# Expert blocks of three and of four token tiles in a routed feed-forward layer

## The chip, the core and the metric

The kernel runs on one core of a Trainium2 chip, as one program. Its time is the device time in microseconds from start to end, and lower is better. The core has five engines with a queue of instructions each: TensorE (PE, with its weight loads shown apart as PEld), VectorE (DVE), ScalarE (ACT), GpSimd (POOL) and SyncE (SP). They wait for one another by semaphores. PSUM, where TensorE writes, has eight banks of 512 fp32 columns.

## The reference

A graph layer is followed by a feed-forward layer with eight experts, of which each token takes one. The change touches the second alone:

```python
T = 20000 tokens, D = 256, F = 1024, E = 8
C = ceil(1.25 * T / E)                                # 3125 places of an expert
logits = layernorm(x) @ gate_w + gate_b
idx = argmax(softmax(logits));  prb = its probability
pos = (cumsum(one_hot) * one_hot).sum(-1) - 1         # rank of a token in its expert
kept = pos < C
buf[idx, pos] = layernorm(x) where kept
hmid = relu(einsum('ecd,edf->ecf', buf, w1) + b1)
ybuf = einsum('ecf,efd->ecd', hmid, w2) + b2
out = x + nan_to_num(ybuf[idx, pos] * (prb * kept))
```

How many tokens an expert gets depends on the data. A token tile is 128 tokens, so an expert has at most 25 of them.

## The kernel before

The program has three stages: edges and nodes (to about 380 us), routing (to about 550 us) and the experts.

**Routing** works over 160 node tiles. VectorE counts how many tokens each expert got, turns this into a number of tiles per expert, and that into a number of blocks. With `BT = 3`, an expert with `t` tiles gets `t // 3 + 1` blocks (`tiles_43`, `tiles_third`: times 43, shifted right by 7), the first `3 * blocks - t` of which are narrow and hold two tiles, the others wide with three. An expert is raised to `LEAST_TILES = 8` tiles, and 9 become 10. `first_block` holds where each expert begins, `first_wide` where its wide blocks begin. A slot table has `NST` slots, `BT` for each of the `NB` blocks that there can be at most, 64 x 3 = 192. It is built in ten steps (`in_row`, `in_tile`, `in_code` on VectorE, then 16 matmuls into `ps_code` on TensorE) and becomes `idx_row` (which rows each slot gathers) and `put_row` (which rows it is added to). Slots without a token read a spare row and are added to spare rows.

**The experts** (`expert_block`) run one loop over narrow blocks and one over wide ones for each expert, with bounds that are read from the two tables. Each matrix is held as a sum of a high and a low part, so a product takes three matmuls. In a block `b`:

- GpSimd (one loop over all blocks) gathers block `b + 2`: for each of `BT` tiles an indirect DMA for the rows (`xg`) and one for their statistics and probability (`sg`). It starts when ScalarE has taken the last ones. Then it adds block `b - 1` to the output, `BT` indirect DMAs (`add_rows`). It does this for all `BT` tiles, in narrow blocks too.
- TensorE does the up projection `up`, for each of 8 slices `f` six matmuls over all the block's columns into one of four `ps_h` banks (`SLOTS = 4`), then the down projection `down` in four steps `j`, for each tile six matmuls of 256 columns into `ps_y`. After the first step it transposes the next block (`turn`, `2 * BT` transposes).
- ScalarE empties each `ps_h` bank twice (`h_hi` and `h_all`, with relu and bias). Between the slices it scales the previous block's rows (`scale_rows`, after `f = 1`) and normalises the next block (`normalise`, after `f = 3`), and at the end takes `x_hi`, the high part of the transposed rows.
- VectorE makes `h_lo` from `h_all - h_hi` for each pair of slices, `x_lo`, and replaces infinities and NaNs of the block before (`find_infinite`, `add_infinities`, `keep_finite`); `add_infinities` waits until the earlier `add_rows` has landed. Last it adds `ps_y` and the bias into `y_sum`.

In each expert's first wide block ScalarE and VectorE also split the next expert's weights in high and low parts (`split_high`, `split_own`, `split_low`).

A narrow block leaves out the third tile in `up`, `down`, the relus, `h_lo` and `y_sum` alone.

## Time and profile before

| | us |
|---|---|
| median of 3 runs | 1450.41 |
| lowest and highest | 1445.53, 1452.19 |
| profiled execution | 1453.49 |
| its span (first to last instruction) | 1451.7 |
| TensorE busy in it | 1221.9 (84%) |
| GpSimd busy | 1016.1 (70%) |
| VectorE busy | 1004.8 (69%) |
| ScalarE busy | 957.3 (66%) |

### The profile page before, as it was taken

The page shows a single profiled execution, that of the slowest core. Times are in us where ns is not written, and L with a number is a line of the kernel's source. Part 1 is how long each engine was busy: PE and PEld are TensorE (multiplying, and loading weights), DVE is VectorE, ACT ScalarE, POOL GpSimd, SP SyncE. Part 2 cuts the span into 40 slices and gives each one's busy share as a digit, 9 for nine tenths or more (in the row PEclk, how much of TensorE's full clock was granted, in tenths as well). Part 3 has the DMA queues.
Part 4 walks back from the last instruction along what each step waited for, and adds up shares of the span by engine and source line. Part 5 has one row for each costly group of instructions (what it writes and reads, how often), then busy time and mean ns, then how long its engine had stood idle before and what let it go on. Part 6 is the DMA issues. An engine that isn't in the chain of part 4 may idle for free.

```text
span 1451.7 us, 26791 instructions
## 1 busy us (share of the span) xinstructions
PE 1221.9 (84%) x7872; PEld 1070.8 (74%) x7872; DVE 1004.8 (69%) x2147; ACT 957.3 (66%) x2128; POOL 1016.1 (70%) x920
## 2 busy tenths in 40 slices
PE   2477678887499343999999999999999999999993
PEld 0244335555366143999999999999999999999993
DVE  7999997986499893755757655755755575556653
ACT  4788896885266363766767666766666776667662
POOL 7788688766477304777777766777776777778785
PEclk9977767999799676999999999999999999999997
DMA  9889976444666202423433422433422342233333
GB/s 331 236 266 284 287 203 145 72 70 49 163 218 216 93 10 84 106 47 48 103 48 55 105 44 47 104 52 49 107 47 44 48 109 48 47 45 55 51 55 41
DMA packets 131884, 153.54 MB, mean 106 GB/s; under 512 B 17164, under 2 KB 118604, under 8 KB 131680
## 3 DMA queue, kind: packets, MB, share of 16 engines
q0 software_dynamic: 51648, 64.60, 27.2%
q1 hardware_dynamic: 58512, 66.59, 14.2%
q10 hardware_dynamic: 21648, 21.49, 4.3%
q8 instruction: 29, 0.48, 0.1%
q14 instruction: 47, 0.39, 0.1%
HBM read 98.82 MB, written 53.81 MB: 105 GB/s over the span
## 4 chain that ended last, share of the span: by engine, by line
PE 52%; issue 4%; POOL 3%; ACT 2%; DMA 1%; DVE 0%; ACTq 0%; POOLq 0%; DVEq 0%
PE f_ps_y L1580 25%; PE f_ps_h L1568 24%; PE f_ps_x L1558 2%; POOL out L1459 1%; POOL xg L1441 1%; POOL sg L1445 1%; ACT h_all L1508 0%; ACT h_hi L1507 0%; DMA sg<-stat_rows,idx_row 0%; DMA sg<-stat_rows,idx_now 0%; ACT f_xn L1492 0%; ACT y_all L1518 0%; DMA out<-clean,put_now 0%; DVE h_lo L1618 0%; ACT w_hi L1335 0%
## 5 line engine op out<-in xcount | busy, mean ns | idle before, releaser
L1507 ACT ACTIVATE h_hi<-f_ps_h,c_b 128x384 fp32r<-128x384 f32 (+1 forms) x416 | 237.2, 570 | 262.9 <-PE f_ps_h L1568 262.9
L1618 DVE TENSOR_TENSOR h_lo<-h_all,h_hi 128x768 fp32r<-128x768 f32 (+1 forms) x208 | 184.1, 885 | 259.2 <-ACT h_all L1508 258.5
L1580 PE MATMUL f_ps_y<-w_hi,h_hi 128*128 128x256 f32 x1136 | 325.1, 286 | 0.7 <-DVE h_lo L1618 0.7
L1580 PE MATMUL f_ps_y<-w_lo,h_hi 128*128 128x256 f32 x1136 | 320.0, 282 | 0.0
L1580 PE MATMUL f_ps_y<-w_hi,h_lo 128*128 128x256 f32 x1136 | 319.9, 282 | 0.0
L1459 POOL DMA_INDIRECT out<-clean,put_now x159 | 263.0, 1654 | 56.8 <-issue 50.0
L1441 POOL DMA_INDIRECT xg<-out,idx_now x159 | 192.9, 1213 | 130.4 <-issue 120.0
L1568 PE MATMUL f_ps_h<-x_hi,w_hi 128*128 128x384 f32 (+1 forms) x832 | 271.8, 327 | 8.1 <-issue 3.5
L1568 PE MATMUL f_ps_h<-x_lo,w_hi 128*128 128x384 f32 (+1 forms) x832 | 269.4, 324 | 0.0
L1568 PE MATMUL f_ps_h<-x_hi,w_lo 128*128 128x384 f32 (+1 forms) x832 | 269.1, 323 | 0.0
L1508 ACT ACTIVATE h_all<-f_ps_h,c_b 128x384 f32<-128x384 f32 (+1 forms) x416 | 238.3, 573 | 0.0
L1445 POOL DMA_INDIRECT sg<-stat_rows,idx_now x159 | 190.6, 1199 | 49.1 <-issue 48.5
L1580 PEld LDWEIGHTS f_ps_y<-w_hi,h_hi 128*128 128x128 f32 x1136 | 213.9, 188 | 1.5 <-DVE h_lo L1618 1.5
L1580 PEld LDWEIGHTS f_ps_y<-w_lo,h_hi 128*128 128x128 f32 x1136 | 214.2, 189 | 0.0
L1580 PEld LDWEIGHTS f_ps_y<-w_hi,h_lo 128*128 128x128 f32 x1136 | 214.2, 189 | 0.0
L1568 PEld LDWEIGHTS f_ps_h<-x_hi,w_hi 128*128 128x128 f32 x832 | 157.2, 189 | 12.6 <-issue 7.4
L1568 PEld LDWEIGHTS f_ps_h<-x_lo,w_hi 128*128 128x128 f32 x832 | 157.2, 189 | 0.0
L1568 PEld LDWEIGHTS f_ps_h<-x_hi,w_lo 128*128 128x128 f32 x832 | 157.2, 189 | 0.0
L418 POOL DMA_INDIRECT out<-rows,upd_row x56 | 98.3, 1755 | 30.3 <-issue 15.5
L582 PEld LDWEIGHTS ps_agg<-same,msg 128*128 128x128 f32 x320 | 68.1, 230 | 67.1 <-issue 57.2
L582 PE MATMUL ps_agg<-same,msg 128*128 128x512 f32 (+3 forms) x320 | 114.2, 519 | 1.6 <-ACT xin L516 1.6
L571 PE MATMUL ps_w<-fc,hidden 64*128 64x320 f32 x160 | 63.8, 552 | 54.4 <-DVE tmp_h L730 53.6
(215 smaller groups left out, 2255.7 us busy)
## 6 DMA issues: line engine op xcount, KB each, us to landing
shared<-out SPq DMA_DIRECT2D x40, 512.0 KB, 3.4
w_raw<-in_w SPq DMA_DIRECT2D x16, 1024.0 KB, 7.4
xin<-in_x SPq DMA_DIRECT2D x24, 512.0 KB, 7.6
out<-xin ACTq DMA_DIRECT2D x24, 512.0 KB, 5.0
shared<-in_x SPq DMA_DIRECT2D x16, 512.0 KB, 5.5
out<-shared ACTq DMA_DIRECT2D x16, 512.0 KB, 5.5
dst_row<-in_dst SPq DMA_DIRECT2D x20, 256.0 KB, 4.6
xg<-out,idx_now POOLq DMA_INDIRECT x159
```

Of the source, the lines that this page charges most:

```text
L418: nc.gpsimd.indirect_dma_start(x1, bass.IndirectOffsetOnAxis(upd_row[:, GT * g + t:GT * g + t + 1].bitcast(U32), 0), rows[g][:, t, :], Non ...
L571: ins = nc.tensor.matmul(ps_w[:, t, :5 * MUL], hidden[:, t * P:(t + 1) * P], fc2[:], start=True, stop=True)
L582: ins = nc.tensor.matmul(ps_agg[:, c, t * P:], msg[g % 2][:, t].rearrange("p u j -> p (u j)")[:, c::2], same[g % 2][t][:], start=t == 0, s ...
L1441: nc.gpsimd.indirect_dma_start(xg[:, i, :], None, out, bass.IndirectOffsetOnAxis(idx[:, i, 0:1].bitcast(U32), 0), bounds_check=ROWS - 1).t ...
L1445: nc.gpsimd.indirect_dma_start(sg[:, i, :], None, io["stat"], bass.IndirectOffsetOnAxis(idx[:, i, 1:2].bitcast(U32), 0), bounds_check=P * ...
L1459: nc.gpsimd.indirect_dma_start(out, bass.IndirectOffsetOnAxis(put_now[:, i:i + 1].bitcast(U32), 0), clean[:, i, :], None, bounds_check=ROW ...
L1507: nc.scalar.activation(h_hi[:, f, :n * P], ps_h[:, f % SLOTS, :n * P], ACT.Relu, bias=b1[:, e, f:f + 1])
L1508: nc.scalar.activation(h_all[f // 2 % 2][:, f % 2, :n * P], ps_h[:, f % SLOTS, :n * P], ACT.Relu, bias=b1[:, e, f:f + 1]).then_inc(h_taken, 1)
L1558: ins = nc.tensor.transpose(ps_x[:, c, i * P:(i + 1) * P], xn[:, i, c * P:(c + 1) * P], ident[:])
L1568: ins = nc.tensor.matmul(ps_h[:, f % SLOTS, :tiles * P], weights[s][:, w], x[:, c, :tiles * P], start=n == 0, stop=n == 5)
L1580: ins = nc.tensor.matmul(ps_y[:, i], x[:, f, i * P:(i + 1) * P], weights[s][:, w], start=i != 1 and f == 0 and n == 0, stop=f == KF - 1 an ...
L1618: tt(h_lo[:, pair, :n * P], h_all[j % 2][:, :, :n * P], h_hi[:, pair, :n * P].bitcast(F32), ALU.subtract).then_inc(h_lo_ready, 1)
```

## The change

The change sets `BT = 4`: wide blocks hold four tiles and narrow ones three. An expert has `t // 4 + 1` blocks. To have at least two wide blocks in each expert, `LEAST_TILES` goes from 8 to 14, and 16 tiles become 17. A four-tile block's `up` matmuls have 512 columns, a whole bank, and `ps_y` is used in full, four tiles of 256 columns in two banks; so the first tile in a bank starts it (`i % 2 == 0`). The number of blocks that there can be at most goes to 51, the slots to 204. In routing the division by four is a shift, with a cast ahead of it; the tile in a narrow block is found by a third of the tile's number, for which a multiplication and a shift take the place of one shift. Everything that ran over `BT` tiles (gathers, `normalise`, transposes, `x_hi` and `x_lo`, `scale_rows`, the clean-up, `add_rows`) now runs over four.

```diff
--- before.py
+++ after.py
@@ -41,11 +41,11 @@
 EPAD = EG * GR
 NEXP, HID = 8, 1024
 CAP = -(-5 * NN // (4 * NEXP))
-BT = 3
+BT = 4
 BR = BT * P
 ET = -(-CAP // P)
-LEAST = 3
-LEAST_TILES = 8
+LEAST = 4
+LEAST_TILES = 14
 
 
 def most_blocks():
@@ -888,8 +888,8 @@
         tiles_sum = sb("tiles_sum", [P, NEXP])
         tiles_least = sb("tiles_least", [P, NEXP])
         tiles = sb("tiles", [P, NEXP])
-        tiles_43 = sb("tiles_43", [P, NEXP], I32)
-        tiles_third = sb("tiles_third", [P, NEXP], I32)
+        tiles_i = sb("tiles_i", [P, NEXP], I32)
+        tiles_fourth = sb("tiles_fourth", [P, NEXP], I32)
         blocks = sb("blocks", [P, NEXP])
         last_block = sb("last_block", [P, NEXP])
         begin = sb("begin", [P, NEXP])
@@ -900,7 +900,8 @@
         own_packed = sb("own_packed", [P, NT], I32)
         own_block = sb("own_block", [P, NT], I32)
         own_narrow = sb("own_narrow", [P, NT], I32)
-        half_i = sb("half_i", [P, NT], I32)
+        high_43 = sb("high_43", [P, NT], I32)
+        third_i = sb("third_i", [P, NT], I32)
         skipped = sb("skipped", [P, NT])
         kept = sb("kept", [P, NT])
         shifted = sb("shifted", [P, NT])
@@ -1211,16 +1212,16 @@
                           thresholds[:].unsqueeze(1).broadcast_to([P, NEXP, ET]), ALU.is_gt))
             chain.link(red(tiles_sum[:], more[:], AX.X, ALU.add))
             chain.link(ts(tiles_least[:], tiles_sum[:], float(LEAST_TILES), None, ALU.max))
-            chain.link(stt(out=tiles[:], in0=tiles_least[:], scalar=9.0, in1=tiles_least[:], op0=ALU.is_equal,
+            chain.link(stt(out=tiles[:], in0=tiles_least[:], scalar=16.0, in1=tiles_least[:], op0=ALU.is_equal,
                            op1=ALU.add))
-            chain.link(ts(tiles_43[:], tiles[:], 43.0, None, ALU.mult))
-            chain.link(ts(tiles_third[:], tiles_43[:], 7, None, ALU.logical_shift_right))
-            chain.link(ts(blocks[:], tiles_third[:], 1.0, None, ALU.add))
+            chain.link(nc.vector.tensor_copy(tiles_i[:], tiles[:]))
+            chain.link(ts(tiles_fourth[:], tiles_i[:], 2, None, ALU.logical_shift_right))
+            chain.link(ts(blocks[:], tiles_fourth[:], 1.0, None, ALU.add))
             chain.mark(stt(out=narrow[:], in0=blocks[:], scalar=float(BT), in1=tiles[:], op0=ALU.mult, op1=ALU.subtract))
             chain.link(nc.vector.tensor_tensor_scan(last_block[:], ones_row[:, :NEXP], blocks[:], 0.0,
                                                     ALU.mult, ALU.add))
             chain.link(tt(begin[:], last_block[:], blocks[:], ALU.subtract))
-            chain.link(stt(out=begin_narrow[:], in0=begin[:], scalar=4.0, in1=narrow[:], op0=ALU.mult, op1=ALU.add))
+            chain.link(stt(out=begin_narrow[:], in0=begin[:], scalar=8.0, in1=narrow[:], op0=ALU.mult, op1=ALU.add))
             chain.mark(ts(begin_high[:], begin_narrow[:], float(RANKS), None, ALU.mult))
             chain.mark(nc.vector.tensor_copy(first_block[:, 1:], last_block[:1]))
             chain.mark(nc.vector.memset(first_block[:, :1], 0))
@@ -1240,14 +1241,15 @@
             chain.wait(2)
             chain.mark(stt(out=kept[:], in0=rank_i[:], scalar=float(CAP), in1=valid[:], op0=ALU.is_lt, op1=ALU.mult))
             chain.mark(ts(high_i[:], rank_i[:], 7, None, ALU.logical_shift_right))
-            chain.mark(ts(half_i[:], rank_i[:], 8, None, ALU.logical_shift_right))
-            chain.wait(3)
-            chain.mark(ts(own_narrow[:], own_packed[:], 3, None, ALU.bitwise_and))
-            chain.mark(ts(own_block[:], own_packed[:], 2, None, ALU.logical_shift_right))
-            chain.wait(4)
+            chain.wait(2)
+            chain.mark(ts(own_narrow[:], own_packed[:], 7, None, ALU.bitwise_and))
+            chain.mark(ts(own_block[:], own_packed[:], 3, None, ALU.logical_shift_right))
+            chain.wait(2)
+            chain.link(ts(high_43[:], high_i[:], 43.0, None, ALU.mult))
+            chain.link(ts(third_i[:], high_43[:], 7, None, ALU.logical_shift_right))
             chain.link(stt(out=shifted[:], in0=kept[:], scalar=-1000.0, in1=low_i[:], op0=ALU.mult, op1=ALU.add))
             chain.mark(ts(slot_row[:], shifted[:], 1000.0, None, ALU.add))
-            chain.link(tt(skipped[:], half_i[:], own_narrow[:], ALU.min))
+            chain.link(tt(skipped[:], third_i[:], own_narrow[:], ALU.min))
             chain.link(stt(out=begin_tile[:], in0=own_block[:], scalar=float(BT), in1=high_i[:], op0=ALU.mult, op1=ALU.add))
             tt(slot_tile[:], begin_tile[:], skipped[:], ALU.add).then_inc(slots_ready, 1)
             v.wait_ge(slots_ready, 1)
@@ -1543,7 +1545,7 @@
             for e in range(NEXP):
                 start, wide, end = bounds(act, e)
                 with act.Fori(start, wide) as b:
-                    step(e, b, 2)
+                    step(e, b, BT - 1)
                 step(e, wide, BT, 1 - e % 2 if e + 1 < NEXP else None)
                 with act.Fori(wide + 1, end) as b:
                     step(e, b, BT)
@@ -1578,8 +1580,8 @@
                         w = slice(W1 + f * D, W1 + (f + 1) * D)
                         for n, (x, weights) in enumerate(((h_hi, w_hi), (h_hi, w_lo), (h_lo, w_hi))):
                             ins = nc.tensor.matmul(ps_y[:, i], x[:, f, i * P:(i + 1) * P], weights[s][:, w],
-                                                   start=i != 1 and f == 0 and n == 0,
-                                                   stop=f == KF - 1 and n == 2 and i > 0)
+                                                   start=i % 2 == 0 and f == 0 and n == 0,
+                                                   stop=f == KF - 1 and n == 2 and (i % 2 == 1 or i == tiles - 1))
                 return ins
 
             def step(e, b, tiles):
@@ -1600,7 +1602,7 @@
             for e in range(NEXP):
                 start, wide, end = bounds(pe, e)
                 with pe.Fori(start, wide) as b:
-                    step(e, b, 2)
+                    step(e, b, BT - 1)
                 with pe.Fori(wide, end) as b:
                     step(e, b, BT)
 
@@ -1676,7 +1678,7 @@
             for e in range(NEXP):
                 start, wide, end = bounds(v, e)
                 with v.Fori(start, wide) as b:
-                    step(e, b, 2)
+                    step(e, b, BT - 1)
                 step(e, wide, BT, 1 - e % 2 if e + 1 < NEXP else None)
                 with v.Fori(wide + 1, end) as b:
                     step(e, b, BT)
```

GpSimd's loop over the blocks, its body as the program has it. Before:

```order
L1472 ISA
L1441 DMA xg<-out,idx_now 128x256
L1445 DMA sg<-stat_rows,idx_now 128x4
L1441 DMA xg<-out,idx_now 128x256
L1445 DMA sg<-stat_rows,idx_now 128x4
L1441 DMA xg<-out,idx_now 128x256
L1445 DMA sg<-stat_rows,idx_now 128x4
L1459 DMA out<-clean,put_now 21504x256 x3
L1472 REGISTER_ALU
```

And now:

```order
L1474 ISA
L1443 DMA xg<-out,idx_now 128x256
L1447 DMA sg<-stat_rows,idx_now 128x4
L1443 DMA xg<-out,idx_now 128x256
L1447 DMA sg<-stat_rows,idx_now 128x4
L1443 DMA xg<-out,idx_now 128x256
L1447 DMA sg<-stat_rows,idx_now 128x4
L1443 DMA xg<-out,idx_now 128x256
L1447 DMA sg<-stat_rows,idx_now 128x4
L1461 DMA out<-clean,put_now 21504x256 x4
L1474 REGISTER_ALU
```

A round has one pair of gathers and one store more, twelve indirect DMAs in place of nine, in front of narrow and of wide blocks alike.

TensorE, where an expert's narrow loop ends and its wide loop begins. Before:

```order
L1580 MATMUL f_ps_y<-w_hi,h_lo 128x256
L1602 REGISTER_ALU
L1602 COMPARE_AND_BRANCH
L1604 UNCONDITIONAL_BRANCH
L1588 REGISTER_ALU
L1563 ISA
L1568 MATMUL f_ps_h<-x_hi,w_hi 128x384
```

And now:

```order
L1582 MATMUL f_ps_y<-w_hi,h_lo 128x256
L1604 REGISTER_ALU
L1604 COMPARE_AND_BRANCH
L1606 UNCONDITIONAL_BRANCH
L1590 REGISTER_ALU
L1565 ISA
L1570 MATMUL f_ps_h<-x_hi,w_hi 128x512
```

The order is the same; the up matmul behind the branch has 512 columns in place of 384.

VectorE in routing, where the slot of each token is worked out. Before:

```order
L1242 TENSOR_SCALAR high_i<-rank_i 128x160
L1243 TENSOR_SCALAR half_i<-rank_i 128x160
L1245 TENSOR_SCALAR own_narrow<-own_packed 128x160
L1246 TENSOR_SCALAR own_block<-own_packed 128x160
L1248 SCALAR_TENSOR_TENSOR shifted<-kept,low_i 128x160
```

And now:

```order
L1243 TENSOR_SCALAR high_i<-rank_i 128x160
L1245 TENSOR_SCALAR own_narrow<-own_packed 128x160
L1246 TENSOR_SCALAR own_block<-own_packed 128x160
L1248 TENSOR_SCALAR high<-high_i 128x160
L1249 TENSOR_SCALAR third_i<-high 128x160
L1250 SCALAR_TENSOR_TENSOR shifted<-kept,low_i 128x160
```

One step is gone from among steps that overlap, and two stand in series behind it (`high` is `high_43`, whose number the listing leaves out).

## Rows read from the trace of the kernel before

**Rows 1.** The page, busy tenths and granted clock in 40 slices.

```profile
PE   2477678887499343999999999999999999999993
PEclk9977767999799676999999999999999999999997
```

**Rows 2.** Busy time by stretch: us, PE, PEld, DVE, ACT, POOL, clock, DMA share, GB/s.

```profile
570.60:1427.70 857.10, 849.20 (x6216) 843.88 (x6216) 516.38 (x759) 576.73 (x1328) 634.35 (x469) 1.00 0.35 63
1290.70:1331.00 40.30, 38.05 (x308) 36.90 (x308) 22.70 (x38) 28.68 (x75) 31.05 (x24) 1.00 0.38 56
```

**Rows 3.** Groups by shape: count | busy us, mean ns | idle before and releasers.

```profile
L1580 PE MATMUL f_ps_y<-w_hi,h_hi 128*128 128x256 f32 x1136 | 325.1, 286 | 0.7 <-DVE h_lo L1618 0.7
...
L1568 PE MATMUL f_ps_h<-x_hi,w_hi 128*128 128x384 f32 x608 | 205.5, 338 | 0.0
...
L1568 PE MATMUL f_ps_h<-x_hi,w_hi 128*128 128x256 f32 x224 | 66.3, 296 | 8.1 <-issue 3.5 <-ACT h_all L1508 2.4 <-DVE x_lo L1613 2.1
```

**Rows 4.** Chain of waits: start us, us, what; starts of experts, one wide block.

```profile
570.60 7.70 PE f_ps_h L1568 x48
...
673.49 0.99 PE f_ps_h L1568 x6
...
757.44 2.41 PE f_ps_h L1568 x18
...
835.73 8.45 PE f_ps_h L1568 x48
844.18 2.16 PE f_ps_y L1580 x18
846.99 6.41 PE f_ps_y L1580 x54
853.40 8.45 PE f_ps_h L1568 x48
...
906.91 2.42 PE f_ps_h L1568 x18
```

**Rows 5.** Groups by shape, the seventh expert alone (1290.7 to 1366.4 us).

```profile
L1568 PE MATMUL f_ps_h<-x_hi,w_hi 128*128 128x256 f32 x48 | 14.0, 291 | 1.0 <-ACT h_all L1508 0.6 <-issue 0.5
...
L1568 PE MATMUL f_ps_h<-x_hi,w_hi 128*128 128x384 f32 x32 | 10.9, 341 | 0.0
```

**Rows 6.** TensorE's timeline in routing: start us, us, what.

```profile
470.02 0.64 PE L1101 MATMUL banks<-xt_lo,r_gate_parts 128*8 128x512 f32 x2
470.49 1.04 PE L1088 MATMUL banks<-c_ident,shared 128*128 128x128 f32 x8
```

**Rows 7.** Waits from 570 to 1428 us: us in total, times, longest.

```profile
PE f_ps_h L1568 <- ACT h_all L1508: 2.4, 13, 0.2
```

**Rows 8.** ScalarE's and VectorE's timelines in the wide block of rows 4.

```profile
841.98 0.22 ACT L1485 COPY idx_now<-idx_row 128x6 int32 x1
842.07 1.61 ACT L1492 ACTIVATE f_xn<-xg,sg 128x256 f32<-128x256 f32 x3
...
845.70 0.96 DVE L1618 TENSOR_TENSOR h_lo<-h_all,h_hi 128x768 fp32r<-128x768 f32 x1 [2.58 <-ACT h_all L1508]
```

**Rows 9.** GpSimd's timeline, the same wide block and the run of narrow ones.

```profile
844.79 1.09 POOL L1441 DMA_INDIRECT xg<-out,idx_now  x1 [2.92 <-issue]
...
1299.27 1.11 POOL L1441 DMA_INDIRECT xg<-out,idx_now  x1 [2.44 <-issue]
...
1307.60 1.63 POOL L1459 DMA_INDIRECT out<-clean,put_now  x1 [0.30 <-issue]
...
1313.79 1.10 POOL L1441 DMA_INDIRECT xg<-out,idx_now  x1 [0.31 <-issue]
```

**Rows 10.** Groups by shape: the ten compares of the slot table.

```profile
L1267 DVE TENSOR_TENSOR in_tile<-iota_q,slot_tile 128x3072 bf16<-128x3072 bf16 x10 | 17.5, 1749 | 0.0
```

**Rows 11.** VectorE's timeline in routing, one linked step.

```profile
507.67 0.32 DVE L1250 TENSOR_TENSOR skipped<-half_i,own_narrow 128x160 f32<-128x160 int32 x1
```

**Rows 12.** Groups by shape: a third of the up projection's weight loads.

```profile
L1568 PEld LDWEIGHTS f_ps_h<-x_hi,w_hi 128*128 128x128 f32 x832 | 157.2, 189 | 12.6 <-issue 7.4 <-ACT h_all L1508 5.1
```

## The prediction

> **What bounds the kernel now.** I read the page first, then the busy time of the expert stretch, then the groups of instructions kept apart by shape, then the chain of waits, and last each engine's own timeline in one wide and one narrow block. The page's slices read 9 for TensorE from the eighteenth of the forty to the last but one, at a granted clock of 9 tenths [rows 1]. The stretch from the first expert matmul (570.6 us) to the last (1427.7 us) is 857.1 us, 59% of the span; TensorE is busy for 849.2 us of it, GpSimd for 634 [rows 2]. So this stretch is TensorE's, and whatever the change does to the columns that TensorE streams it does to the time.
>
> The stretch consists of 52 blocks. Every block has 16 of the `w_hi, x_hi` matmuls of the up projection: 608 with 384 columns are 38 wide blocks, 224 with 256 columns are 14 narrow ones, and 1136 down matmuls of one kind are 142 token tiles at 8 each [rows 3]. A wide block is the clean pattern of the chain: 8.45 us up (48 matmuls, 0.176 us each), 2.16 + 6.41 us down (72 matmuls, 0.1190 us each), 0.65 us between these two for the six transposes, 17.67 us from one block to the next, no gap [rows 4]. A narrow block would be 5.72 + 5.72 + 0.65 = 12.1 us by the same pace. The distance between the starts of two experts gives each expert's plan. The first, from 570.60 to 673.0, takes 102.4 us: one narrow block (14.0, the first of all) and five wide ones, 17 tiles. (Later experts' first matmuls come after a gap of 0.5 us, which I count to the block.) Second: 83.9 us, one narrow (13.2) and four wide, 14 tiles. Third: 149.5 us, two narrow (25.8 together) and seven wide, 25 tiles. The fourth repeats the second, the fifth and sixth repeat the third [rows 4]. The seventh shows 48 and 32 up matmuls, three narrow and two wide blocks, 12 tiles [rows 5]; two narrow and two wide are left for the last, 10 tiles. Sum 142.
>
> **The change part by part.** First the plan. The new rule is tiles / 4 rounded down, plus one block, and as many narrow blocks as tiles are short of four each; but every expert is raised to 14 tiles at least (8 before). The 17, 14 and 25 stay (none is 16, which would grow), the 12 and the 10 become 14. This gives blocks (narrow, wide): 5 (3, 2), 4 (2, 2), 7 (3, 4), 4 (2, 2), 7 (3, 4), 7 (3, 4), 4 (2, 2), 4 (2, 2). Together 42 blocks, 20 of three tiles and 22 of four, 148 tiles: **ten blocks fewer, six tiles more**.
>
> Next the price of a block on TensorE. A three-tile block is measured: 8.45 + 8.57 us, and eight transposes in place of six, 0.65 x 8/6 = 0.87: 17.9 us. A four-tile block has 96 down matmuls, 11.43 us, the transposes 0.87, and 48 up matmuls of 512 columns. These 512-column matmuls on 128 stationary columns are in no row. Three bounds: the step from 256 to 384 columns, 0.119 to 0.176 us, taken once more gives 0.233; the same step at one column per cycle of 2.4 GHz would be 0.053, 0.229; the routing stage has 512-column matmuls of the same type with 8 stationary columns, a pair of which starts 0.47 us before what follows it, 0.235 each [rows 6]. I take 0.233, 11.2 us, since two of the three meet there; a four-tile block is 23.5 us (23.3 to 23.6). Filling the bank thus buys next to nothing: per tile the up projection costs 2.86 us at 256 columns, 2.82 at 384 and 2.80 at 512.
>
> Sum of the stretch: 22 x 23.5 + 20 x 17.9 = 875 us. What comes on top: the gap at the first block of an expert, 3.5 us in all [rows 3], which no edit touches; the slower first block, about 1.4 us (14.0 against 13.2 less the gap), kept; 1 us for GpSimd, below. 881 us, **+24 us** against 857.1.
>
> The old narrow blocks cost more than 12.1 us, 186 us for 14 where 169 would be the pace. Their waits are for ScalarE, 13 of them [rows 7]: a two-tile up projection fills a slot every 0.71 us, faster than ScalarE, with `scale_rows` in between, empties them. In the new narrow block TensorE fills a slot every 1.06 us, as in the old wide one, which had no wait. What is new for ScalarE there is a fourth tile in `scale_rows` and in `normalise`, by a tile of `xn` up to 0.5 us each (1.61 us for three), before its fifth relu. The relus of the third pair feed an `h_lo` that starts at 845.70 in a block begun at 835.73 and takes 0.96 [rows 8]: ready 10.9 us into the block, wanted by the down projection at 13.4. One microsecond more leaves 1.5. I cost this at nothing; were that cover gone, each narrow block would wait for up to 0.5 us, 10 us at most. Of the 17 us by which the old narrow blocks exceed their pace, the sum has all but 5 as gone.
>
> **GpSimd** is the cover to watch. It issues 3 x (xg, sg) and 3 x out per block; the change makes both fours, empty tiles included. Where it was not waiting, one round took 14.5 us (1299.27 to 1313.79), gathers 8.3 to 9 and stores 5.8 to 6.2 [rows 9], 4.85 us a tile, so 19.4 to 19.6 us a round of four. That is over the 17.9 us of a narrow block and under the 23.5 of a wide one: each narrow block lags by some 1.6 us, each wide one recovers nearly 4. From the wide block: gathers begin at 844.79 after a wait of 2.9 us, are all issued some 9 us later, near 854, and the next `normalise` wants them at 859.65, 17.67 after 841.98 [rows 8, 9]. Less about 1.5 for landing, a lag of some 4 us has room in a three-tile rhythm; runs of three narrow blocks make up to 2 x 1.6 = 3.2 by the third. I count 1 us for the four runs together, with 0 and 10 as ends. Queued behind a late GpSimd are ScalarE (`normalise` waits for the gathers, then the relus) and VectorE (`add_infinities` waits for the stores to land, behind it `y_sum`).
>
> **Ahead of the stretch** everything is in series: one more xg and sg before the first transposes, 2.8 us by the gathers above; one more tile of `xn` 0.5; two transposes 0.4; `x_hi` and `x_lo`, a third wider, 0.5: +4.2. In routing, the plan has 204 slots in place of 192: ten compares of 1.75 us grow by a sixteenth [rows 10], +1.1 on VectorE, which TensorE waits for there, and the divide by three of the tile number puts two linked steps of about 0.3 us [rows 11] in place of one that the next overlaps, +0.4. Together **+5.7 us**.
>
> **Behind it:** GpSimd's last round starts about 11.2 us into the last block in place of 9.1, while the block ends 5.8 later, so the tail begins 3.7 us earlier against TensorE's end. It has one gather pair more (3.0), one store more of each of the last two blocks (3.8), and a third more of `clean`'s two passes on VectorE (0.65, at about a microsecond each now): +7.4, net **+3.7 us** on the 24.0 between 1427.7 and the span's end.
>
> Sum: 24 + 5.7 + 3.7 = **+33 us**. The profiled execution took 1453.5 us (its span 1451.7), 3 us over the median of the runs; on its own time it becomes 1487, on the median of 1450.4 it becomes **1484 us**, 2.3% slower. In short: the six empty tiles cost 6 x 5.7 = 34 us, and what the fewer blocks save (narrow waits, about 11 us, and little else) is eaten by ends that got longer.
>
> The Trainium skill speaks for another result. TensorE: Matmul & The Clock Gate, section Back-to-back issue gap, gives for a stream of weight loads and matmuls a sustained spacing of about 131 ns at 512 columns and 81 ns at 128, and an isolated gap of 512/2.4 + 2.5 = 216 ns. By the first, 1056 matmuls would each be 0.10 us cheaper than in my sum. The trace does not agree: this kernel's stream already stands at 176 ns with 384 columns [rows 4].
>
> **Rivals.**
> (a) As summed: TensorE at its pace, GpSimd's lag absorbed. 1478 to 1491 us.
> (b) GpSimd's round becomes the bound in the narrow runs. For it: 19.5 against 17.9 us, and in the old run of three narrow blocks GpSimd, after 2.4 us in front of its first gather, goes from round to round without a pause, and the three take 40.3 us for 36.3 of pace [rows 2, 9]. Against: wide blocks follow each run. Unabsorbed, the second and third narrow blocks cost 1.6 us each, 12 blocks, 19 us: 1494 to 1503 us.
> (c) The 512-column matmul streams at 2.4 GHz without the surplus of 12 to 16 ns that 256 and 384 columns show, 0.213 us: 1056 x 0.020 = 21 us less, 1463 us. Still slower than before.
> (d) The other side: a matmul into a full bank costs no more than one of 384 columns, because its weight load, recorded with 189 ns [rows 12], and not its columns sets the pace. Place: `up` in the 22 wide blocks; price: 1056 x (0.233 - 0.189) = 46 us less, 1438 us. It decides from a pace of 0.208 us on, below which the kernel is not slower. Against it: the down matmuls have a weight load of the same length each and stand at 0.119 us, so loads do not set the pace. By the sustained figure of the Trainium skill's section above it would even be 1484 - 108 = 1376 us, an estimate.
> (e) The plan isn't what I read: the two short experts not raised to 14. Then 142 tiles, 1450 us. The code leaves no room, but the counts will show it.
>
> **How the numbers follow.** (a) 0.82, (b) 0.11, (c) 0.03, (d) 0.02, (e) and anything else near no change 0.02. The predicted time is (a)'s. The range has to leave out (c), (d), (e) and half of what is odd about the unknown costs: below, 1484 less 4 for cheaper 512-column matmuls, less 1 for GpSimd, less 4 for the ends and 2 for the spread of the runs; above it takes in (b). 1473 to 1502 us. Faster by over 0.5% has 0.02, within 0.5% 0.02, slower by over 0.5% 0.96; half a per cent, 7 us, is about what a measurement of this kernel can tell from no change.
>
> **What would show it.** In the groups: 352 `w_hi, x_hi` matmuls with 512 columns and 320 with 384, 1184 down matmuls of a kind; any other count and the plan is wrong. In the chain: 11.2 us for 48 up matmuls of a wide block, 23.5 us from block to block; 17.9 in a narrow one after the first of its expert. From the first expert matmul to the last: 881 us, starting 5 us later in the span. GpSimd: rounds of 19.5 us, its wait before the gathers 3 to 4 us in wide blocks and gone in the third narrow one. The tail behind TensorE: 28 us in place of 24. I am wrong if the 512-column matmul stands below 0.21 us, if narrow blocks take over 19 us, or if the transposes or the relus show waits in them.

## The result, and the profile after

| | before | after |
|---|---|---|
| median | 1450.24 (4 runs) | 1495.73 (4 runs) |
| lowest and highest | 1445.53, 1452.19 | 1490.77, 1497.36 |
| profiled execution, its span | 1453.49, 1451.7 | 1494.48, 1492.7 |
| first expert matmul to the last | 857.1 | 891.1 |
| behind the last matmul | 24.0 | 30.8 |

The changed kernel takes 1.0313 of the time before, 95% interval 1.0277 to 1.0348: slower by 45.5 us. The two profiled executions lie 41.0 us apart, since the one of before was 3.25 us over its median and the one of after 1.25 under.

The page of the changed kernel, TensorE's slices and the chain's shares by engine:

```profile
PE   2577678884898237999999999999999999999991
PEclk9977769997899587999999999999999999999996
PE 38%; issue 10%; POOL 10%; ACT 2%; DMA 2%; DVE 0%; POOLq 0%; ACTq 0%; DVEq 0%
```

TensorE still reads 9 through the stretch, as in [rows 1]. What is new is GpSimd's share in the chain that ended last: 10% of the span, where it had 3% before, and its own issue gaps beside it (issue 10%, before 4%); TensorE's share fell from 52% to 38%. The groups, shapes apart (busy us, mean ns of one | idle before, releaser), first TensorE's, then GpSimd's:

```profile
L1582 PE MATMUL f_ps_y<-w_hi,h_hi 128*128 128x256 f32 x1184 | 339.1, 286 | 0.7 <-DVE h_lo L1620 0.7
L1570 PE MATMUL f_ps_h<-x_hi,w_hi 128*128 128x512 f32 x352 | 138.9, 395 | 0.0
L1570 PE MATMUL f_ps_h<-x_hi,w_hi 128*128 128x384 f32 x320 | 110.4, 345 | 6.1 <-issue 3.6 <-DVE x_lo L1615 2.6
...
L1461 POOL DMA_INDIRECT out<-clean,put_now x172 | 295.4, 1717 | 58.2 <-issue 48.8 <-DVE clean L1647 6.1 <-ACT prob_next L1499 3.4
L1447 POOL DMA_INDIRECT sg<-stat_rows,idx_now x172 | 223.6, 1300 | 53.2 <-issue 53.2
L1443 POOL DMA_INDIRECT xg<-out,idx_now x172 | 219.8, 1278 | 72.5 <-issue 62.6 <-ACT prob_next L1499 9.9
```

352 / 16 = 22 wide blocks, 320 / 16 = 20 narrow ones, 1184 / 8 = 148 tiles: the plan is the predicted one, where [rows 3] gave 38, 14 and 142. The chain in a wide block in the middle of an expert (start, us, what, count):

```profile
838.63 11.14 PE f_ps_h L1570 x48
849.77 2.88 PE f_ps_y L1582 x24
852.64 0.87 PE f_ps_x L1560 x8
853.52 8.64 PE f_ps_y L1582 x72
862.15 0.92 PE f_ps_h L1570 x4
```

11.14 / 48 = 0.232 us for a matmul of 512 columns, and 23.5 us from block to block, beside 0.176 and 17.67 in [rows 4].

The rest of the stretch is not this clean. The chain across the first expert's third narrow block shows it:

```profile
614.86 1.30 POOL xg L1443
616.17 0.30 issue
616.47 2.33 DMA sg<-stat_rows,idx_now
619.00 0.16 ACT idx_now L1487
...
620.13 1.05 ACT f_xn L1494 x2
621.23 1.09 PE f_ps_x L1560 x8
622.32 6.40 PE f_ps_y L1582 x54
```

The last gather of the fourth tile is issued at 616.47. ScalarE can't normalise before it has landed, and TensorE waits for the transposes. In the list of waits (us in total, times, longest) this is

```profile
ACT idx_now L1487 <- DMA sg<-stat_rows,idx_now: 38.7, 20, 3.6
PE f_ps_x L1560 <- ACT f_xn L1494: 26.3, 5, 21.2
DVE put_now L1641 <- DMA out<-clean,put_now: 18.7, 16, 7.7
```

The same two of before:

```profile
PE f_ps_x L1558 <- ACT f_xn L1492: 21.0, 2, 19.8
...
ACT idx_now L1485 <- DMA sg<-stat_rows,idx_now: 13.6, 13, 2.0
```

TensorE's long one lies in front of the stretch in both. The others are now four and 5.1 us together: the four third narrow blocks.

The blocks, from one block's first matmul to the next one's, for the profiled execution of after (the last block of all, which has none behind it, is left out):

| | us | pace |
|---|---|---|
| wide, not last of an expert, 12 | 23.41 to 23.59 | 23.5 |
| narrow, second of an expert | 17.87 to 17.90 | 17.9 |
| first of an expert, seven | 17.96 to 18.07 | 17.9 |
| last of an expert, the gap to the next included, seven | 24.09 to 24.30 | 23.5 + 0.65 |
| narrow, third of an expert, four | 19.35, 19.40, 19.55, 19.30 | 17.9 |
| wide behind a run of narrow ones, two of eight | 24.28, 24.53 | 23.5 |
| the very first | 20.52 | 17.9 |

22 x 23.53 + 20 x 17.88 = 875.3. Gaps and firsts of an expert are 5.4, the very first block 2.6, and what is left, 7.7, is the third narrow blocks (6.1) and two wide blocks (1.7): GpSimd.

### The profile page after: what moved, and what is told of

It reads as the page before. It is cut to its first block, busy times and chain, and to the rows that moved or that the text cites. A ratio compares the mean times of both kernels' runs of the same rounds, so it can differ in the third digit from the quotient of the medians.

```text
span 1492.7 us, 25220 instructions
## 1 busy us (share of the span) xinstructions
PE 1252.6 (84%) x7562; PEld 1059.0 (71%) x7562; DVE 1015.2 (68%) x2018; ACT 956.9 (64%) x1964; POOL 1121.2 (75%) x961
## 4 chain that ended last, share of the span: by engine, by line
PE 38%; issue 10%; POOL 10%; ACT 2%; DMA 2%; DVE 0%; POOLq 0%; ACTq 0%; DVEq 0%
PE f_ps_h L1570 19%; PE f_ps_y L1582 17%; POOL xg L1443 4%; POOL out L1461 3%; POOL sg L1447 3%; PE f_ps_x L1560 2%; DMA sg<-stat_rows,idx_now 1%; ACT f_xn L1494 1%; ACT h_hi L1509 0%; ACT h_all L1510 0%; DMA sg<-stat_rows,idx_row 0%; DMA out<-clean,put_now 0%; DVE h_lo L1620 0%; ACT w_hi L1337 0%; POOLq L1447 0%
## 5 line engine op out<-in xcount | busy, mean ns | idle before, releaser
L1509 ACT ACTIVATE h_hi<-f_ps_h,c_b 128x512 fp32r<-128x512 f32 (+1 forms) x336 | 215.7, 642 | 269.9 <-PE f_ps_h L1570 268.0
L1620 DVE TENSOR_TENSOR h_lo<-h_all,h_hi 128x1024 fp32r<-128x1024 f32 (+1 forms) x168 | 184.1, 1096 | 273.6 <-ACT h_all L1510 273.6
L1461 POOL DMA_INDIRECT out<-clean,put_now x172 | 295.4, 1717 | 58.2 <-issue 48.8
L1447 POOL DMA_INDIRECT sg<-stat_rows,idx_now x172 | 223.6, 1300 | 53.2 <-issue 53.2
L1570 PE MATMUL f_ps_h<-x_hi,w_hi 128*128 128x512 f32 (+1 forms) x672 | 249.3, 371 | 6.1 <-issue 3.6
L1570 PE MATMUL f_ps_h<-x_lo,w_hi 128*128 128x512 f32 (+1 forms) x672 | 248.2, 369 | 0.0
L1570 PE MATMUL f_ps_h<-x_hi,w_lo 128*128 128x512 f32 (+1 forms) x672 | 248.0, 369 | 0.0
L1510 ACT ACTIVATE h_all<-f_ps_h,c_b 128x512 f32<-128x512 f32 (+1 forms) x336 | 216.1, 643 | 0.0
L1570 PEld LDWEIGHTS f_ps_h<-x_hi,w_hi 128*128 128x128 f32 x672 | 127.4, 190 | 22.6 <-issue 7.9
L1570 PEld LDWEIGHTS f_ps_h<-x_hi,w_lo 128*128 128x128 f32 x672 | 127.4, 190 | 15.3
```

What stands on the lines that cost most here:

```text
L1447: nc.gpsimd.indirect_dma_start(sg[:, i, :], None, io["stat"], bass.IndirectOffsetOnAxis(idx[:, i, 1:2].bitcast(U32), 0), bounds_check=P * ...
L1461: nc.gpsimd.indirect_dma_start(out, bass.IndirectOffsetOnAxis(put_now[:, i:i + 1].bitcast(U32), 0), clean[:, i, :], None, bounds_check=ROW ...
L1509: nc.scalar.activation(h_hi[:, f, :n * P], ps_h[:, f % SLOTS, :n * P], ACT.Relu, bias=b1[:, e, f:f + 1])
L1510: nc.scalar.activation(h_all[f // 2 % 2][:, f % 2, :n * P], ps_h[:, f % SLOTS, :n * P], ACT.Relu, bias=b1[:, e, f:f + 1]).then_inc(h_taken, 1)
L1570: ins = nc.tensor.matmul(ps_h[:, f % SLOTS, :tiles * P], weights[s][:, w], x[:, c, :tiles * P], start=n == 0, stop=n == 5)
L1620: tt(h_lo[:, pair, :n * P], h_all[j % 2][:, :, :n * P], h_hi[:, pair, :n * P].bitcast(F32), ALU.subtract).then_inc(h_lo_ready, 1)
```

## The experiments

Every set stands beside runs of the kernel before on the same chip. The second and third set ran on two chips on which the kernel before took 1449.7 us (13 runs) and 1449.3 us (7 runs); their times are compared with each other. The first set ran on a chip on which it took 1516.4 us (9 runs, 1511.6 to 1524.1). There the order of the kernels was another, so all four of that set were run again, and I tell first what the later sets show.

### The changed kernel again

> The changed kernel as it is, so that the experiments can be compared with it under the same conditions. If the +45 us of the first comparison belong to the change alone, it is 1.031 of the kernel before here too. If what differed in the first set of experiments (there the kernel before took 1516 in place of 1450 us, and kernels with blocks of four tiles stood at 0.985 to 1.007 of it) is a cost of the loops' changes, which the kernel before has as often with more blocks between, the ratio depends on the chip: between 0.99 and 1.01 where the kernel before takes about 1516 us, and 1.031 where it takes 1450.

1494.8 us, 1.033 (1.0293 to 1.0366). The same as in the first comparison.

### Six tiles more, in the old blocks

```diff
--- before.py
-LEAST_TILES = 8
+LEAST_TILES = 14
```

> The kernel before with its least number of tiles at 14: blocks of two and three tiles, but 148 tiles as in the changed kernel. By the prediction's prices the six added tiles are 6 x 5.65 to 5.9 = 34 to 35 us and the waits in the narrow blocks, two of which go, give back 1 to 3: +31 us, ratio 1.021 to 1.024 where the kernel before takes 1450 us. Rival, that the change's cost is mainly in its blocks of four (GpSimd's longer rounds, ends): under +20 us.

1482.7 us, 1.0231 (1.019 to 1.0271), +33.0 us; by the interval it is 28 to 39. The stretch is 887.8 us in place of 857.1, +30.7, and the tail 24.5 in place of 24.0. So some 33 of the 45 us have nothing to do with blocks of four: they are the empty tiles of the two short experts. The prediction had 34 for them, this run's own expectation 31. What the blocks of four cost beside that is 12 us (1494.8 - 1482.7).

### A full bank, or two halves

```diff
--- after.py
-ins = nc.tensor.matmul(ps_h[:, f % SLOTS, :tiles * P], weights[s][:, w], x[:, c, :tiles * P],
-                       start=n == 0, stop=n == 5)
+parts = ((0, 2 * P), (2 * P, 4 * P)) if tiles == BT else ((0, tiles * P),)
+for k, (lo, hi) in enumerate(parts):
+    ins = nc.tensor.matmul(ps_h[:, f % SLOTS, lo:hi], weights[s][:, w], x[:, c, lo:hi],
+                           start=n == 0 and k == 0, stop=n == 5 and k == len(parts) - 1)
```

> The changed kernel, but each up matmul of a wide block, 512 columns into a full bank, is issued as two of 256 columns (the same weights loaded twice), 1056 more matmuls. Theory (a matmul's pace is its columns, 0.119 us at 256 and 0.232 at 512, and a full bank is worth nothing by itself): a wide block goes from 23.53 to 48 x 2 x 0.119 + 11.43 + 0.87 = 23.7 us, +0.2 to +0.3 each, +4 to +6 us over 22 blocks, less what of GpSimd's lag the longer blocks absorb: +3 to +6 us against the changed kernel. Rival (fewer and wider matmuls are what the change gives, its cost is elsewhere): +20 us or more.

1494.7 us, 1.0315 (1.0297 to 1.0334): no difference from the changed kernel. Its chain in a wide block:

```profile
860.27 11.39 PE f_ps_h L1572 x96
871.66 2.85 PE f_ps_y L1584 x24
874.50 0.87 PE f_ps_x L1560 x8
875.38 8.53 PE f_ps_y L1584 x72
```

96 matmuls of 256 columns take 11.39 us, 48 of 512 took 11.14: the block is 23.65 in place of 23.53, 2.6 us over 22 blocks. That is all that the full bank is worth, and the stretch (893.2 against 889.3 and 891.1 in the two profiles of the changed kernel) is 2 to 4 us longer; the medians don't resolve it. The theory held, with a smaller price than its 3 to 6 us.

### Three stores a round

```diff
--- after.py, in add_rows; the waits on `written` count three a block
-for i in range(BT):
+for i in range(BT - 1):
```

> The changed kernel with three stores a round in place of four (rows of the fourth tile of each block aren't added to the output; all else is done). GpSimd's round becomes some 17.5 us, under the 17.9 of a narrow block. Theory (its rounds of over 19 us cost some 7 us in the stretch, at the third narrow block of a run): against the changed kernel of this set -7 us in the stretch and -4 behind it, -10 to -12 us. Rival (the stores hide and the third narrow blocks wait for something else): -4 us, from the end alone, and third narrow blocks stay at 19.4.

1481.8 us, 1.0227 (1.0194 to 1.026), 13.0 us less than the changed kernel. This kernel leaves the rows of each block's fourth tile out of the output; it measures GpSimd's part alone. The third narrow blocks stand at 17.94, 18.07, 18.20 and 18.13; the stretch is 883.7 us against 889.3, the tail 24.9 against 30.6. The rival, that third narrow blocks wait for something else, falls. And it puts the blocks of four, once GpSimd keeps up, at the time of the old blocks with as many tiles (1482.7), as far as runs that spread over 4 and 9 us can tell. In the profiles its stretch is 4.1 us shorter than that of the old blocks, and begins 1.4 us later: what blocks of four save is a few microseconds at most, and this kernel has a quarter of the stores left out to get them.

### VectorE's pass over one tile

```diff
--- after.py; clean is set to zero once at the start
-tt(clean[:], positive[:], negative[:], ALU.add).then_inc(infinite_ready, 1)
+tt(clean[:, 0], positive[:, 0], negative[:, 0], ALU.add).then_inc(infinite_ready, 1)
```

> The changed kernel with VectorE's pass clean = positive + negative over one of the four tiles in place of all (the others are set to zero once, so that it is the same for rows without infinities). By the trace a gather takes 1.01 us beside an idle VectorE and 1.9 beside this pass. Theory (contention with VectorE is what makes rounds of gathers 12 to 13.9 us long): the pass shrinks from 1.22 to some 0.35 us, one gather a block becomes 0.7 to 0.9 us shorter, and over a run of three narrow blocks the lag shrinks by 2 us: third narrow blocks at 18.0 to 18.5, -5 to -7 us in the stretch, -1 in the tail. Rival (gathers of four tiles are slow because of their number and order, whatever VectorE does): 0 to -2 us.

1481.6 us, 1.0225 (1.0201 to 1.0249), 13.2 us less than the changed kernel, more than I expected. All third narrow blocks are at 17.86 to 17.89, the stretch is 882.3 us in place of 889.3, the tail 27.8 in place of 30.6, and the waits of ScalarE for a landing gather are gone from the list. The busy time of each engine in the stretch (from:to, us, then PE, PEld, DVE, ACT and POOL with their operations, granted clock, DMA share, GB/s), first of the changed kernel in the second set, then of this one (both windows end 0.2 us ahead of the last matmul's end):

```profile
571.40:1460.50 889.10, 880.68 (x5904) 830.25 (x5904) 523.59 (x629) 575.30 (x1162) 716.89 (x503) 1.00 0.37 64
```
```profile
570.50:1452.60 882.10, 878.46 (x5904) 830.59 (x5904) 490.13 (x629) 574.61 (x1162) 693.33 (x505) 1.00 0.38 65
```

GpSimd, the fifth, is busy for 23.6 us less with as many DMAs, though not one of its instructions was changed. All of it is in the gathers: 1.29 us each on average in the changed kernel and 1.21 here, the stores 1.71 and 1.72. Where it comes from can be read off the timelines. In the last block of the changed kernel (start, us, operation, idle before), a gather beside the pass, one beside the end of the pass that follows, and one beside nothing:

```profile
1455.72 2.00 POOL L1443 DMA_INDIRECT xg<-out,idx_now  x1 [0.30 <-issue]
1458.03 1.20 POOL L1447 DMA_INDIRECT sg<-stat_rows,idx_now  x1 [0.30 <-issue]
1459.53 1.01 POOL L1443 DMA_INDIRECT xg<-out,idx_now  x1 [0.30 <-issue]
```
```profile
1455.62 1.22 DVE L1642 TENSOR_TENSOR clean<-positive,negative 128x1024 f32<-128x1024 f32 x1
```

Which of the two begins first decides. The same place in two profiles of the changed kernel, the fourth gather of a round in an expert's first narrow block, in the first comparison and then in the second set:

```profile
774.90 2.07 POOL L1447 DMA_INDIRECT sg<-stat_rows,idx_now  x1 [0.30 <-issue]
```
```profile
774.86 1.22 DVE L1642 TENSOR_TENSOR clean<-positive,negative 128x1024 f32<-128x1024 f32 x1
```
```profile
775.57 1.01 POOL L1447 DMA_INDIRECT sg<-stat_rows,idx_now  x1 [0.30 <-issue]
```
```profile
775.54 1.28 DVE L1642 TENSOR_TENSOR clean<-positive,negative 128x1024 f32<-128x1024 f32 x1
```

Both gathers are recorded within 0.04 us of the pass's start. In the first profile the gather takes 2.07 us and the pass 1.22; in the second the gather takes 1.01 and the pass 1.28.

In the first comparison's profile, the gathers of the stretch by the VectorE pass that each overlapped longest: 1.89 us on average beside `clean` (33 of them), 1.44 beside `h_lo` (88), 1.25 beside `x_lo` (32), and 1.02 beside no pass (62). The averages mix two cases. All 42 gathers that were issued while this pass ran took what was left of it and 0.88 to 0.91 us more; those issued ahead of it (14) took 1.04. Behind the start of an `h_lo`, with no other pass near, the 48 gathers took what was left of it and 0.88 to 0.97 us; ahead of it, 1.01 to 1.10 us (32). Beside `y_sum`, which has one input in PSUM, all 28 took 1.01 us, wherever they began. In the kernel before it is the same, with 48 gathers behind the start of its `clean` pass, what was left and 0.88 to 0.95 us; there the pass took 0.95 us in place of 1.22.

Both `clean` and `h_lo` have two inputs in SBUF. The Trainium skill, SBUF — State Buffer, section Who interferes with whom, says that a VectorE instruction with two SBUF inputs contends with a GpSimd instruction that reads SBUF; it calls the ports that they share an exclusive lock, for which the order of issue decides who waits. The trace agrees: the gather issued 0.10 us behind the pass is longer by 0.99 us, nearly what was left of the pass (1.12). The same section infers that such a pass does not hold up the making of DMA descriptors; it did hold up these gathers, which are DMAs that GpSimd issues.

In the second set's profile of the changed kernel two of the four third narrow blocks stood at 18.02 and 18.13 and two at 19.49. In the former the gathers began 15.3 and 15.4 us into the block, in the latter 16.8. So a microsecond and a half, which the rounds before gain or lose by whether their gathers and stores run into a pass, decides whether such a block waits. The four lines above are from the run of narrow blocks whose third stood at 19.40 in the one profile and at 18.02 in the other.

### The gathers that nobody uses

```diff
--- after.py; the last two add_rows stand behind the loop, and the last wait counts one round less
-with pool.Fori(0, blocks) as b:
+with pool.Fori(0, blocks - 1) as b:
```

> The changed kernel without GpSimd's last round of gathers, which fetches rows that no block uses. In its tail these eight gathers take 13.4 us and end 2.8 us after TensorE, while VectorE's cleaned rows for the stores behind them are ready at 1458.3. Theory (the tail's growth from 24.0 to 30.9 us is GpSimd's row of gathers): stores begin at about 1460.3 in place of 1464.8, -4 to -5 us in the tail, and nothing before. But the last block's own y_sum, its clean-up (from 1461.95 to 1467.2) and the landing of the stores come next. Rival, by what the same edit did to the kernel before (stores only 0.4 us earlier): -1 us or less.

1487.3 us, 1.0262 (1.0243 to 1.0282), 7.5 us less than the changed kernel; between last matmul and end of the span 24.6 us in place of 30.6 in the second set. The store that follows the gathers in the changed kernel and in this one, and VectorE's wait for the stores to land, first of the changed kernel in the first comparison:

```profile
1464.80 1.88 POOL L1461 DMA_INDIRECT out<-clean,put_now  x1 [0.30 <-issue]
...
1478.47 1.57 POOL L1461 DMA_INDIRECT out<-clean,put_now  x1 [6.10 <-DVE clean L1647]
```
```profile
1474.87 0.17 DVE L1641 COPY put_now<-put_row 128x4 int32 x1 [7.67 <-DMA out<-clean,put_now]
```

then without the unused gathers:

```profile
1458.70 1.55 POOL L1461 DMA_INDIRECT out<-clean,put_now  x1 [8.15 <-DVE clean L1648]
...
1472.29 1.56 POOL L1461 DMA_INDIRECT out<-clean,put_now  x1 [6.16 <-DVE clean L1648]
```
```profile
1468.69 0.17 DVE L1642 COPY put_now<-put_row 128x4 int32 x1 [2.04 <-DMA out<-clean,put_now]
```

The last stores start 6.2 us earlier, 5.6 us when counted from the last matmul's end. The theory holds; it asked for 4 to 5. The tail's growth was GpSimd's row of gathers, with the stores queued behind it.

### Three tiles less

```diff
--- after.py; 12 and 13 tiles become 14
-LEAST = 4
-LEAST_TILES = 14
+LEAST = 3
+LEAST_TILES = 11
```

> The changed kernel with the least number of tiles at 11 (12 and 13 still become 14), so that the last expert has 11 tiles in place of 14: one narrow and two wide blocks. Three empty tiles and one block less. By the price of a narrow block, 17.9 us, and with the lag of the last pair of narrow blocks unchanged: -17.9 us against the changed kernel, ratio 1.020 to 1.022 of the kernel before where that takes 1450. Rival (most of the change's cost is in blocks of four as such): less than -10 us.

1475.7 us, 1.0185 (1.0163 to 1.0207), 19.1 us less. The stretch is 874.0 us, and 17.9 more would be 891.9, where the changed kernel has 889 to 891. One narrow block costs what its pace says, and the rival falls.

### Two edits on the kernel before

```diff
--- before.py; besides, the last gathers left out as above
 if f == 1:
-    scale_rows(b - 1)
...
+    scale_rows(b - 1)      # after f == 3, before normalise
...
-if j == 0:                 # next_prob, find_infinite
+if j == 1:
```

> The kernel before with two edits that the traces suggest. First, GpSimd's last round no longer gathers rows that no block uses (the gathers of its last two rounds are for blocks behind the last): the tail becomes 3 x 2.85 = 8 us shorter for GpSimd, of which 5 to 6 us end up in the time since the last block's own end comes next. Second, ScalarE scales the previous block's rows after the fourth relu in place of the second and VectorE cleans one step later, so that ScalarE doesn't leave TensorE without a free bank in blocks of two tiles: 13 waits of 2.4 us in the count of waits and some 5 to 8 us in blocks of two tiles. Theory: -11 us, 0.992 of the kernel before. Rival (the waits only move to normalise, which then stands against the relus behind it): -5 us.

1452.0 us, 1.0018 (0.9999 to 1.0036): nothing gained, and both expectations missed. The first narrow block of an expert went from 12.6 to 12.3 us, but the second from 12.5 to 12.7, and the five wide ones behind a run of narrow ones took 91.1 us together in place of 89.7; the stretch was 858.1 in place of 857.1. The waits in a narrow block were moved, not removed. In the tail (start, us, idle before):

```profile
1428.06 1.55 POOL L1459 DMA_INDIRECT out<-clean,put_now  x1 [8.65 <-DVE clean L1645]
...
1438.94 1.55 POOL L1459 DMA_INDIRECT out<-clean,put_now  x1 [5.43 <-DVE clean L1645]
```

Without the gathers these stores wait 8.65 us for VectorE's clean-up, which the other edit had put later, and begin at 1428.06, where before they began at 1428.46. The last ones begin at 1438.94, before at 1439.43. Counted from the last matmul's end the tail is 21.9 us in place of 24.0, so 2.1 us were gained there, and the stretch took 1.0 back. That GpSimd's gathers were nearly hidden here, as they were not with blocks of four, is likely but not shown, since the two edits were made together and the other one moved the clean-up that these stores wait for.

### The first set, on another chip

The same kernels as four of those above, with the kernel before at 1516.4 us.

> The kernel before (blocks of two and three tiles) with every expert raised to 14 tiles in place of 8, so that it computes the same 148 tiles as the changed kernel. Theory A, TensorE pays for empty tiles as for full ones: the seventh and eighth expert each become one narrow and four wide blocks, 83.9 us each by the second expert, in place of 75.7 and 61.3, so +31 us, 1481 us; what is left to the changed kernel's 1495.7, about 15 us, is then the price of the block form (GpSimd's lag, slower start and end). Rival B, the form of the blocks carries all of the loss and empty tiles hide in waits: 1450 to 1456 us.

1536.9 us, 1.0135 (1.0092 to 1.0178), +20.5 us where the later set had +33.0.

> The changed kernel with 11 tiles allowed as the least (12 and 13 become 14, 16 becomes 17): only the last expert changes, from 14 tiles in two narrow and two wide blocks to 11 in one narrow and two wide, 145 tiles in all. Theory A: one three-tile block of TensorE less, 18 us, and two short steps more in routing, so 1478 us against 1495.7. Rival B (empty tiles cost little): 1490 us or more.

1495.7 us, 0.986 (0.9828 to 0.9892), where the later set had 1.0185.

> The changed kernel with GpSimd adding only the first three of four tiles to the output in each round; a quarter of the feed-forward result is left out, nothing else. A round gets shorter by one store, about 1.9 us, from 20 to 18 us. Theory A (GpSimd's lag is what made the third narrow blocks take 19.4 us in place of 17.9 and the wide block behind them up to a microsecond too long, about 8 us in all, and it makes the last round start late): narrow blocks all at 17.9 us, the tail behind TensorE shorter by 4 to 6 us, 1482 to 1485 us. Rival C (the long blocks have another cause, such as ScalarE's or VectorE's wider work): the third narrow blocks stay at 19.4 us and only the tail gets shorter, 1491 to 1493 us.

1492.8 us, 0.9851 (0.9804 to 0.9898), where the later set had 1.0227.

> The changed kernel with VectorE's sum of the two infinity parts made for the first of four tiles only (all of this data is finite, so the rest of that sum is zero anyway); one 1.2 us pass of VectorE per block becomes 0.35 us. Theory D (indirect DMAs are issued more slowly by GpSimd while VectorE runs a pass that reads two operands from SBUF; beside this pass gathers take 1.9 us in place of 1.01): two gathers per round get 0.8 us shorter, rounds go from 20 to some 18.4 us, third narrow blocks to 18 us, and the whole gains 7 to 10 us, 1486 to 1489 us. Rival E (a slow gather is slow by its own traffic, whatever VectorE does): gathers stay as they are, gain 1 us or less, 1495 us.

1526.5 us, 1.0073 (1.0039 to 1.0106), where the later set had 1.0225.

So on this chip two of the three kernels with blocks of four were 1.4 to 1.5% faster than the kernel before, and the third was 0.7% slower. Against the later sets they had lost 20, 11 and 45 us; of the old blocks, the kernel before had lost 67 and the one with 148 tiles 54. Where the time goes can be seen by laying the two profiles of the 148 tiles in old blocks side by side. Its stretch is 937.6 us in place of 887.8. 42 of its 53 blocks have the same length to 0.3 us; eleven don't. Ten of them are the block behind an expert's first narrow one or the first wide one, where the loop jumps back or changes, and one is a third wide block: 18.5 to 22.8 us in place of 12.5 or 17.7, in sum some 49 us. There ScalarE comes late, not TensorE. The first relu in the first expert's first wide block, begun at 587.99, in the first set, and in the second set, begun at 585.00:

```profile
592.77 0.58 ACT L1507 ACTIVATE h_hi<-f_ps_h,c_b 128x384 fp32r<-128x384 f32 x1 [7.14 <-PE f_ps_h L1568]
```
```profile
586.42 0.58 ACT L1507 ACTIVATE h_hi<-f_ps_h,c_b 128x384 fp32r<-128x384 f32 x1 [4.40 <-PE f_ps_h L1568]
```

4.8 us into the block, against 1.4. And in the first set's waits there are rows that the second set's list doesn't have, waits of ScalarE and VectorE for nothing that the profile shows:

```profile
ACT h_hi L1507 <- issue: 47.0, 8, 6.9
DVE y_sum L1673 <- remote: 25.2, 10, 5.2
DVE h_lo L1618 <- issue: 17.1, 8, 4.2
```

In the kernel with three stores a round only the first narrow block of an expert is longer there (19.0 to 19.5 in place of 17.95 to 18.07), about 8 us in the stretch, and with the quarter pass it is again other blocks. The Trainium skill, Runtime: NRT & Kernel Launch, section Instruction fetch mechanics, says that a taken branch whose target is outside the two pages held makes the engine wait until the page is fetched. That would fit the places; no run here measured such a fetch by itself. The instruction queues don't decide it: both profiles move the same 29 and 47 packets in them, and the sixteen of 16 KB in the stretch took 1.10 us on average in the slower profile and 1.13 in the other, so the packets themselves weren't slower. What made it slower in this set, whether it was the chip itself, and why other loop bodies suffer in other programs, stays open. I did not run the changed kernel there. By its distance in the later sets to the three kernels that differ little from it (19 us to that with 11 tiles, 13 to that with three stores, 13 to that with the quarter pass) it would take 1515, 1506 or 1540 us, 0.993 to 1.015 of the kernel before: an estimate. So "3% slower" holds for the first comparison and for the chip of the second set, and probably not for this one, where even the sign is open.

## Why the prediction was right, and where its sum was off

The forecast was 1484 us, 1473 to 1502; it came out at 1495.7. The sign and the main term held; the point was 12 us too low. The time lies where rival (b) put it (1494 to 1503), but that is in part luck: (b) asked for 1.6 us in each of twelve narrow blocks, 19 us, and only the four third ones waited, 1.4 to 1.7 us each, with two wide blocks behind; the second ones kept their 17.9. GpSimd's part in the stretch was 7.7 us, and the rest of the miss has other causes.

- **The plan**: 42 blocks, 148 tiles, as read. Rival (e) is out.
- **Six empty tiles, 34 us**: 33.0 by the old blocks with 148 tiles (28 to 39 by the interval).
- **The 512-column matmul**, 0.233 us from the step between two shapes: 0.232. Rivals (c) and (d) are out. The Trainium skill's 131 ns sustained at 512 columns (TensorE: Matmul & The Clock Gate, section Back-to-back issue gap), which by an estimate would have given 1376 us, does not hold for this stream; with 1056 matmuls twice as narrow the time stayed the same.
- **Pace of the blocks**, 23.5 and 17.9: 23.53 and 17.88, and no relu or transpose wait in an ordinary narrow block; the fourth tile in `scale_rows` and `normalise` was hidden, as costed.
- **The gaps at an expert's first block**, 3.5 us in all: 5.4. I took half a microsecond each from a group's total of waits; the block lengths give 0.65 (18.32 against 17.67, before as well) and 0.13 more in the block behind. The view with the distances would have said so. 2 us. The reading of the old narrow blocks was off as well, without effect on the sum: the fourteen take 184 us with their gaps, not 186, so they exceed their pace by 14.5 us, not 17. And in rival (d), 0.208 us is the pace at which the kernel would be half a per cent slower; no slower it is from 0.201 us on.
- **The first block**, 1.4 us: 2.6. TensorE begins it at half clock in both kernels, and it lasted longer here. By the windows below (last but two: granted clock), first of the kernel before, then of the changed one, the clock was at 0.50 until 574.5 us before, 3.9 us into the stretch, and until 576.4 in the changed kernel, 5.6 us in:

```profile
573.00:576.00 3.00, 3.00 (x22) 3.00 (x22) 0.86 (x2) 2.63 (x8) 2.02 (x2) 0.75 0.17 44
```
```profile
573.00:576.00 3.00, 3.00 (x11) 3.00 (x10) 0.00 (x0) 1.90 (x4) 2.39 (x3) 0.50 0.17 45
576.00:579.00 3.00, 3.00 (x17) 3.00 (x17) 2.03 (x4) 3.00 (x8) 1.77 (x2) 0.93 0.25 44
```

  Half of 5.6 us is 2.8, near the 2.6. The second set's profile of the changed kernel shows that this differs from run to run: half clock ended 3.4 us into the stretch and the first block took 19.47, 1.6 over its pace; but the second took 18.92, with ScalarE waiting 2.4 us for a gather there.

- **GpSimd, 1 us in the stretch, with 0 and 10 as ends: the step that was mis-sized**, at 7.7 us. The mechanism, the place (the last block of a run of narrow ones) and the two ends were right. The size was not, because I scaled a round by its tiles, 4.85 us each. From one round's first gather to the next one's it took 21.2 to 22.4 us at an expert's first block and, in the runs of three, 19.8 to 20.0 at the second, for 17.9 of the blocks. So the gathers begin 10.2 to 11.0 us into the first block of a run and 16.6 to 16.8 into the third: a lag of 6 us where I had 3.2. What I hadn't weighed is that VectorE's passes get a third longer too, and that a gather issued while one with two SBUF inputs runs waits for its end. That this counts, the quarter pass shows: -7 to -9 us in the stretch. The prediction's own sign of being wrong, narrow blocks of over 19 us, showed in these four of the twenty.
- **Ahead of the stretch, 5.7 us**: from VectorE's `best` to the first expert matmul 89.2 us in place of 85.6, +3.7; the wait for the last gather to land was 2 us shorter than before. But the stretch began only 0.2 us later (570.8 against 570.6), since `best` itself, which no edit touches, came 3.5 us earlier. This wasn't one execution's luck: on the undisturbed chips it stands at 484.3 to 485.3 in three profiles with blocks of three, and at 478.7 to 481.6 in seven with blocks of four. On the chip of the first set there was no such difference: 487.4 with blocks of three, 487.3 to 488.2 in three profiles with blocks of four. I have no cause for it. That it took most of the late start away was luck.
- **The tail, 3.7 us**: 6.8. The last round of gathers began 13.1 us into the last block in place of 11.2 and took 13.4 us in place of some 12: GpSimd's lag once more. Without that round the tail is 24.6 us.

In spans: 0.2 + 34.0 + 6.8 = +41.0, 8 us more than the sum of 33. GpSimd has 10 of the excess, in the stretch (6.7) and in the tail (3.1), and the gaps and the first block 3; the earlier start took 5.5 away. Either of two edits that shorten GpSimd's rounds gives back 13 us. The other 4 us between 1484 and 1495.7 are that the profiled execution of before stood 3 us over its median and the one of after 1 under.

The costs can be taken back one by one (-19 us for three of the six tiles, -13 for the lag, -7.5 for the unused gathers), but even if they all added up the time would be near 1455 us, still not under the kernel before, and the last two overlap, since each shortens the tail; with the fuller bank worth 2.6 us and the tiles costing 5.65 each, there is nothing in the change to pay for the rest. That combination was not run, nor was a round that leaves out the gathers of a narrow block's empty tile.

## What to carry to other kernels

Where a matmul's pace follows its columns, a fuller bank saves next to nothing: here 2.6 us in all, and one tile of empty work costs 5.65. An engine with 25 to 30% slack by its busy share can still set the time in the stages where its round is longer than the others': compare round with round in the shortest block, and give each operation the duration that it has beside what will run next to it. Look also at which of the two begins first: a difference of hundredths of a microsecond turned a gather of 1.01 us into one of 2.07. And a difference of a few per cent that hangs on the number of loop changes should be measured on more than one chip.
